# A gate factor held in a ScalarE register, and the o gate's seed copied by VectorE, in a graph layer followed by an LSTM-like cell

## The chip, the cores and the metric

The kernel runs on one core of one Trainium2 chip. The metric is the device time in microseconds of one execution. Before the change the median of three runs is 478.73 us (477.65 to 478.92). One execution was profiled; its span, from the first to the last instruction of the core, is 477.4 us.

## The reference

The input x is 3125 rows of 256 numbers. First comes a graph layer: normalise each row, multiply by a 256 by 256 weight, add a bias, average over the neighbours given by 53,125 (source, destination) pairs, and add to x. Then comes a recurrent cell over the rows as one sequence; its output is added to x again. The cell is what the change touches:

```
i = sigmoid(x_t U_i + b_i + h V_i)      g = tanh(x_t U_c + b_c + h V_c)
o = sigmoid(x_t U_o + b_o + h V_o)
c_new = h * c + i * g                   h_new = o * tanh(c_new)
```

## The kernel before

The 3125 rows are cut into 125 chunks of 25 rows, and the cell advances all 125 chunks side by side: one step of the kernel is one row of every chunk. As the chunks depend on each other only through their ends, the kernel runs 24 early steps with less exact products (`HIDDEN = 24`), mixed into the work of the graph layer, and then 41 full turns (`t` from 25 to `DONE` = 65). At the end a test compares two states and would start a slow path if they did not agree.

A sigmoid is computed as a tanh with halved weights, so all gates use one function. The weights are scaled by a power of two before they are split in two fp16 halves, and each gate's tanh has to undo this factor: it is in the third column of the small tensor `w_unscale`, the same number in all 128 partitions.

In a full turn the 125 chunks are two halves, q = 0 (63 chunks) and q = 1 (62 chunks), which follow each other half a turn apart. I call the work of one half in one turn a half-turn; there are 82. The names and lines of a half-turn, engine by engine:

- TensorE (L1351, function `full_products`): 36 matmuls. The state h is split as hi + lo in fp16. The first 16 take hi for the gates i and g, then 2 for the first part of o, then a wait for `lo_ready`, then 8 matmuls with lo that end i and g (`ig_ps`, these are the 19th to the 26th), then 10 that end o (`o_ps`). The i and g sums of half q are in PSUM bank `ps_g[q]`, the o sum in `ps_x[q]`, four different banks. In the last 25 turns a half-turn also has a transpose of an older state for the output (L1387).
- ScalarE: `gate_ig` (L1024, tanh of i and g, waits for `ig_ps`), `gate_o` (L1032, waits for `o_ps`), `seed_ig` (L1011) and `seed_o` (L1017), which copy the inputs' share `gx` of the half's next turn into the PSUM banks so that the matmuls add to it, and `cell_tanh` (L1038, waits for the new cell `c_ready`).
- VectorE: `new_part` (L1813, i times g, waits for `gate_ig` and for the product h * c), `state_low` of the other half (L1861, writes lo), `cell` (L1819), in the last 25 turns `add_out` (L1883, adds a transposed state to the output), then `state_next`: hi (L1824, output h, waits for the cell's tanh) and the full state (L1824, output h_flat).
- GpSimd: the product h * c (L778).

The order on each engine is that of the Python code; nothing reorders it. In the early steps the gates are L959, for all 125 chunks at once.

The o seed has its place behind both gates and behind the seed of i and g:

Of the kernel before, what the change touches and what calls it, by code (L numbers as in the profile page):

```python
# [6 lines left out]
I32 = mybir.dt.int32  # L7
# [3 lines left out]
ACT = mybir.ActivationFunctionType  # L11
# [14 lines left out]
HIDDEN = 24  # L26
# [7 lines left out]
def bass_gnn_lstm_kernel(nc, x, src, dst, dst_src, w_gnn, b_gnn, U_i, V_i, b_i, U_c, V_c, b_c, U_o, V_o, b_o, out):  # L34
# [4 lines left out]
    HH = H // P  # L39
# [19 lines left out]
    MT = 3 * HH  # L59
# [3 lines left out]
    COLS = [(0, (CHUNKS + 1) // 2), ((CHUNKS + 1) // 2, CHUNKS)]  # L63
# [22 lines left out]
    with ExitStack() as ctx:  # L86
        def sb(name, shape, dt=F32):
            return ctx.enter_context(nc.sbuf_tensor(name, shape, dt))
# [4 lines left out]
        def sem(name):  # L93
            return ctx.enter_context(nc.semaphore(name))
# [8 lines left out]
        gx = gx_flat[:, 0:STEPS * MT * CHUNKS].rearrange("p (s m k) -> p s m k", s=STEPS, m=MT)  # L103
# [89 lines left out]
        w_unscale = sb("w_unscale", [P, 3])  # L193
# [37 lines left out]
        ps_x = [bank[2], bank[3]]  # L231
# [42 lines left out]
        unscales_ready = sem("unscales_ready")  # L274
# [42 lines left out]
        e_gate = sem("e_gate")  # L317
# [20 lines left out]
        o_seed = [sem(f"o_seed{i}") for i in range(2)]  # L338
        ig_gate = [sem(f"ig_gate{i}") for i in range(2)]
        o_gate = [sem(f"o_gate{i}") for i in range(2)]  # L340
# [20 lines left out]
        DONE = 3 * STEPS - RUN * FIRST_GROUP  # L361
# [17 lines left out]
        def at_gx(t):  # L379

            return (t - 1) % STEPS
# [63 lines left out]
        def batch_of(b):  # L445

            return (b // TB, b % TB) if b < TB * PAIRS else (b - PAIRS * (TB - 1), 0)
# [389 lines left out]
        def _(act):  # L837
# [37 lines left out]
            def counts_out(w):  # L875
# [6 lines left out]
                if i == HOT_WINDOWS - 1 and g >= 2:  # L882
# [4 lines left out]
                                         "p (n r t) -> p r t n", n=n, r=RUN),  # L887
                                     ACT.Copy).then_inc(counted, 1)

            act.wait_ge(consts, 1)  # L890
            nc.scalar.activation(sd[0:1, 0:1], ones[0:1, 0:1], ACT.Sqrt).then_inc(table_set, 1)
            act.wait_ge(scales_ready, 1)
            nc.scalar.activation(W16[:, 0, :, :], w_sb[:, 0:DH * D].rearrange("p (d h) -> p d h", d=DH), ACT.Copy,
                                 scale=w_scale[:, 0:1]).then_inc(w_hi, 1)
            nc.scalar.activation(b16[:, :], w_sb[0:B_LOW + 1, DH * D:(DH + 1) * D], ACT.Copy,
                                 scale=w_scale[0:B_LOW + 1, 0:1]).then_inc(b_hi, 1)
# [58 lines left out]
            def early_gate(t, m0, m1):  # L955
                act.wait_ge(e_ps, 2 * t - (1 if m0 == 0 else 0))
                if m0 > 0 and t >= SHARP:
                    act.wait_ge(e_h, t - SHARP + 1)
                nc.scalar.activation(gate_w[:, m0:m1, :],  # L959
                                     ps_early[:, 0:(m1 - m0) * CHUNKS].rearrange("p (m k) -> p m k", k=CHUNKS),  # L960
                                     ACT.Tanh, scale=w_unscale[:, 2:3]).then_inc(e_gate, 1)

            def early_tanh(t):
                of, to = early_cols(t)
# [6 lines left out]
            for w in range(PLACES_END):  # L971
                if w + WINDOWS < NW:
                    counts_out(w + WINDOWS)
                if w == 97:
                    nc.scalar.activation(tc[0:1, 0, 0, 0:1], ones[0:1, 0:1], ACT.Tanh).then_inc(table_set, 1)
                if w in UV_HIGH:
                    if w == UV_HIGH[0]:
                        act.wait_ge(scales_ready, 2)
                    n, u, w_from, w16 = uv_parts[UV_HIGH.index(w)]
                    nc.scalar.activation(w16[:, 0, :, n * H:(n + 1) * H], w_from[:, :, n, :], ACT.Copy,  # L980
                                         scale=w_scale[:, 1 + u:2 + u]).then_inc(uv_hi, 1)
                t = early_turn(w, E_SEED)
                if t:
                    early_seed(t, 0, 2 * HH)
                t = early_turn(w, E_GATE)
                if t:
                    early_gate(t, 0, 2 * HH)
                    early_seed(t, 2 * HH, MT)
                t = early_turn(w, E_OUT_GATE)
                if t:  # L990
                    early_gate(t, 2 * HH, MT)
                t = early_turn(w, E_TANH)
                if t:
                    early_tanh(t)
                for _, (j0, j1), u in gates_at(w, out=True):
                    gates_out(j0, j1 - j0)
                t = block_at(w, HIGH_AT)
                if t is not None:
                    act.wait_ge(z2T_ps, t + 1)
                    batch, at_b = batch_of(t)  # L1000
                    if batch >= 2 and at_b == 0:
                        act.wait_ge(gx_ps, UNITS * (batch - 1))
                    nc.scalar.activation(z2T[:, batch % 2, 0, :, at_b, :],
                                         ps_zT[:, 0:DH * NB].rearrange("p (d n) -> p d n", d=DH),
                                         ACT.Copy).then_inc(z2T_hi, 1)
# [8 lines left out]
            def seed_o(q, s):  # L1014
                c0, c1 = COLS[q]
                n = c1 - c0
                nc.scalar.activation(ps_x[q][:, 0:HH * n].rearrange("p (m k) -> p m k", k=n),  # L1017
                                     gx[:, bass.ds(s, 1), 2 * HH:MT, c0:c1], ACT.Copy).then_inc(o_seed[q], 1)

            def gate_ig(q, turn):  # L1020
                c0, c1 = COLS[q]
                n = c1 - c0
                act.wait_ge(ig_ps[q], turn)
                nc.scalar.activation(gate[:, q, 0:2 * HH, 0:n],  # L1024
                                     ps_g[q][:, 0:2 * HH * n].rearrange("p (m k) -> p m k", k=n), ACT.Tanh,
                                     scale=w_unscale[:, 2:3]).then_inc(ig_gate[q], 1)

            def gate_o(q, turn):
                c0, c1 = COLS[q]
                n = c1 - c0  # L1030
                act.wait_ge(o_ps[q], turn)
                nc.scalar.activation(gate[:, q, 2 * HH:MT, 0:n],  # L1032
                                     ps_x[q][:, 0:HH * n].rearrange("p (m k) -> p m k", k=n), ACT.Tanh,
                                     scale=w_unscale[:, 2:3]).then_inc(o_gate[q], 1)

            def cell_tanh(q, turn, c, c0, c1):
                act.wait_ge(c_ready[q], turn)
# [8 lines left out]
            for t in range(HIDDEN + 1, DONE + 1):  # L1046
                n = t - HIDDEN

                def next_ig(q):
                    if t < DONE:  # L1050
                        act.wait_ge(ig_gate[q], n)
                        seed_ig(q, at_gx(t + 1))

                def tanh_c(q):
                    cell_tanh(q, n, c_after(t), *cols_after(t, q))

                for q in range(2):
                    gate_ig(q, n)
                    gate_o(q, n)
                    next_ig(q)  # L1060
                    if t < DONE:
                        act.wait_ge(o_gate[q], n)
                        seed_o(q, at_gx(t + 1))
                    tanh_c(q)

            def general_block(j):
# [387 lines left out]
        def _(dve):  # L1454
# [318 lines left out]
            for w in range(PLACES_END):  # L1773
# [15 lines left out]
                if w in UV_LOW:  # L1789
                    n = UV_LOW[w]  # L1790
                    m, u, w_from, w16 = uv_parts[n]
# [5 lines left out]
                t = early_turn(w, E_CELL)  # L1797
                if t:
                    early_cell(t)
                t = early_turn(w, E_STATE)  # L1800
                if t:
                    early_state(t)
                t = early_turn(w, E_LOW)
# [23 lines left out]
            def state_next(q, t):  # L1827
# [26 lines left out]
                else:  # L1854
                    state(1, h[:, :, c0:c1], n).then_inc(h_ready[1], 1)

            def state_low(q, t):
                c0, c1 = COLS[q]
                dve.wait_ge(h_ready[q], t - HIDDEN)
                dve.wait_ge(hi_ready[q], t - HIDDEN)  # L1860
                nc.vector.tensor_tensor(h16[:, 1, :, c0:c1], h_after(t)[:, :, c0:c1], h16[:, 0, :, c0:c1],  # L1861
                                        ALU.subtract).then_inc(lo_ready[q], 1)
# [29 lines left out]
            for t in range(HIDDEN + 1, DONE + 1):  # L1892
                n = t - HIDDEN

                def cell_after(q):
                    cell(q, n, c_after(t), *cols_after(t, q))

                if t == LAST_ROUND + 2:
                    dve.wait_ge(x1_stored, 16 * GROUPS_S)
                for q in range(2):  # L1900
                    new_part(q, n)
                    if q == 0 and n > 1:
                        state_low(1, t - 1)
                    elif q == 1 and t < DONE:
                        state_low(0, t)
                    cell_after(q)
                    if (t, q) == (DONE, 1):
                        cell_gap()
                    else:
                        for step, d in out_parts(t, q)[:LAST_OUTS[q]]:  # L1910
                            add_out(step, d)
                    state_next(q, t)
                if n == 1:
                    dve.wait_ge(covered_ps, 1)
                    link(nc.vector.tensor_scalar(open_f[:, :], ps_one[0:1, 0:1], float(E), None, ALU.not_equal))
                    link(nc.vector.tensor_copy(open_i[:, :], open_f[:, :]))
# [127 lines left out]
```

## Time and profile before

| | before |
|---|---|
| median of 3 runs | 478.73 us |
| span of the profiled execution | 477.4 us |
| stage 339.8 to 468.7 us (the full turns) | 128.9 us |
| in it TensorE / ScalarE / VectorE / GpSimd busy | 115.1 / 119.0 / 105.4 / 34.5 us |
| TensorE clock granted over the span | 0.979 |

The file has no time of its own for the profiled execution besides its span; the median of the runs is 1.3 us above that span. Busy times of an engine are sums in which two instructions that overlap count once. An instruction on ScalarE or VectorE may start before the one in front of it has ended, so the distance between two starts is often shorter than the duration of the first. Bracketed notes such as "[0.34 <-PE bank L1351]" give the idle time before an instruction and who ended it. Lines are those of the kernel before.

### The profile page before, as it was taken

To read this page: it belongs to the slowest core of one execution; us is meant where nothing else is said; L and a number is where in the kernel's file an instruction comes from. 1 tells how busy PE (TensorE), PEld (TensorE's weight loads), DVE (VectorE), ACT (ScalarE), POOL (GpSimd) and SP (SyncE) were. 2 spreads that over 40 slices of the span, in tenths; PEclk is the share of its full clock that TensorE was granted. 3 is DMA by queue.
4 is the path that set the end of the run, shared out by engine and by line. 5 is a ranking of instruction groups with operands and counts; after the bars stand their busy time and mean duration, and the time that the engine had idled before them with its cause. 6 is when DMAs were issued, how large, how long until landed. Compare 5 with 4: busy or idle time off the path is not lost.

```text
span 477.4 us, 15480 instructions
## 1 busy us (share of the span) xinstructions
PE 425.7 (89%) x6096; PEld 371.7 (78%) x6096; DVE 356.8 (75%) x1119; ACT 345.6 (72%) x905; POOL 184.8 (39%) x322
## 2 busy tenths in 40 slices
PE   3986988989999999999999999986788889999992
PEld 3674777778888898899988888875677778888882
DVE  4989987897987878778786553345577778888885
ACT  1575786477776777777777755464899989999991
POOL 5730650356454546555464342221122222322320
PEclk9999799999999999999999999997999999999997
DMA  7372001330100001000100010001000000110112
GB/s 190 67 185 84 2 1 43 104 104 24 55 2 1 1 15 42 2 1 7 50 2 2 1 55 1 1 1 56 1 3 3 5 3 4 57 58 3 58 56 61
DMA packets 9604, 16.91 MB, mean 35 GB/s; under 512 B 2006, under 2 KB 7451, under 8 KB 9526
## 3 DMA queue, kind: packets, MB, share of 16 engines
q1 hardware_dynamic: 8230, 14.60, 10.1%
q0 software_dynamic: 880, 0.86, 0.9%
q8 instruction: 50, 0.82, 0.7%
q10 hardware_dynamic: 416, 0.39, 0.3%
q14 instruction: 28, 0.23, 0.2%
HBM read 6.23 MB, written 9.61 MB: 33 GB/s over the span
## 4 chain that ended last, share of the span: by engine, by line
PE 40%; DVE 33%; ACT 13%; issue 7%; POOL 4%; DMA 2%; SPq 0%; DVEq 0%; ACTq 0%
PE bank L1218 9%; PE bank L1220 9%; PE bank L1252 9%; DVE hots L1601 6%; ACT tc L1038 5%; DVE h L1824 5%; DVE h L1861 5%; PE bank L1280 4%; DVE c_st L1819 4%; PE bank L1170 4%; DVE h_flat L1824 3%; POOL newton L744 2%; DMA x_sb<-in_x_dram 2%; ACT counts L885 2%; PE bank L1203 2%
## 5 line engine op out<-in xcount | busy, mean ns | idle before, releaser
L1170 PE MATMUL bank<-hots 128*128 128x125 f16 x625 | 121.1, 223 | 1.7 <-ACT counts L885 1.7
L1351 PE MATMUL bank<-h,V 128*128 128x62 f16 (+1 forms) x2952 | 107.1, 192 | 14.0 <-DVE h L1824 8.7
L1351 PEld LDWEIGHTS bank<-h,V 128*128 128x128 f16 x2952 | 96.4, 97 | 27.9 <-issue 23.3
L1601 DVE TENSOR_TENSOR hots<-iota,kp 128x1024 f16<-128x1024 f16 x160 | 108.9, 710 | 8.8 <-PE bank L1170 8.3
L1218 PE MATMUL bank<-h_flat,counts 125*128 125x257 f16 x375 | 97.2, 273 | 0.4 <-ACT h_flat L873 0.4
L1220 PE MATMUL bank<-h_flat,counts 125*128 125x256 f16 x375 | 96.3, 271 | 0.0
L778 POOL TENSOR_TENSOR hc<-h_flat,c_st 128x126 f32<-128x126 f32 x80 | 34.1, 427 | 97.9 <-DVE c_st L1819 91.5
L885 ACT ACTIVATE counts<-bank 125x500 f16<-125x500 f32 x96 | 55.5, 612 | 19.3 <-PE bank L1170 18.1
L1218 PE MATMUL bank<-h_flat,gx 125*128 125x257 f16 x250 | 68.2, 273 | 0.0
L1220 PE MATMUL bank<-h_flat,gx 125*128 125x256 f16 x250 | 67.4, 270 | 0.0
L1170 PEld LDWEIGHTS bank<-hots 128*128 128x128 f16 x625 | 57.5, 98 | 9.5 <-issue 1.1
L934 ACT ACTIVATE gx<-bank,gb,gx_scale 128x250 f32<-128x250 f32 (+1 forms) x84 | 40.5, 534 | 23.7 <-PE bank L1252 23.6
L1252 PE MATMUL bank<-z2T,U 128*128 128x250 f16 (+1 forms) x504 | 56.7, 261 | 1.0 <-ACT gx L934 0.5
L744 POOL TENSOR_SCALAR newton<-rstd,var_eps 125x1 f32<-125x1 f32 x48 | 30.7, 640 | 66.4 <-DVE rstd L1683 64.0
L885 ACT ACTIVATE gx<-bank 125x500 f16<-125x500 f32 x64 | 37.4, 592 | 19.9 <-PE bank L1170 18.1
L1252 PEld LDWEIGHTS bank<-z2T,U 128*128 128x128 f16 x504 | 44.2, 99 | 6.5 <-issue 1.3
L1218 PEld LDWEIGHTS bank<-h_flat,counts 125*128 125x128 f16 x375 | 36.6, 98 | 4.8 <-issue 0.5
L1824 DVE SCALAR_TENSOR_TENSOR h<-gate,tc 128x126 f16<-128x126 f32 (+1 forms) x80 | 23.6, 295 | 20.6 <-ACT tc L1038 20.6
L1024 ACT ACTIVATE gate<-bank,w_unscale 128x252 f32<-128x252 f32 x82 | 38.5, 470 | 0.3 <-PE bank L1351 0.3
L1220 PEld LDWEIGHTS bank<-h_flat,counts 125*128 125x128 f16 x375 | 36.6, 98 | 1.5
L959 ACT ACTIVATE gate<-bank,w_unscale 128x500 f32<-128x500 f32 (+1 forms) x48 | 27.6, 576 | 13.9 <-PE bank L1280 13.0
L745 POOL TENSOR_SCALAR rstd<-newton,rstd 125x1 f32<-125x1 f32 x48 | 35.7, 744 | 4.9
(169 smaller groups left out, 801.2 us busy)
## 6 DMA issues: line engine op xcount, KB each, us to landing
h_dram<-h_flat SPq DMA_DIRECT2D x1, 3137.2 KB
x_dram<-x_sb SPq DMA_DIRECT2D x5, 625.0 KB
x_sb<-in_x_dram SPq DMA_DIRECT2D x5, 560.0 KB
out_dram<-x_sb SPq DMA_DIRECT2D x4, 560.0 KB
out_dram<-x_sb SPq DMA_DIRECT2D x1, 336.0 KB
x_sb<-in_x_dram SPq DMA_DIRECT2D x5, 65.0 KB
out_dram<-x_sb SPq DMA_DIRECT2D x4, 65.0 KB
gx<-in_L_gnn_weight_dram ACTq DMA_DIRECT2D x1, 256.0 KB, 3.8
```

What stands on the lines that cost most here:

```text
L744: link(nc.gpsimd.tensor_scalar(t, y, v, y, ALU.mult, ALU.mult))
L745: link(nc.gpsimd.tensor_scalar(y, t, -three, y, ALU.add, ALU.mult))
L885: nc.scalar.activation(counts[g % 2][:, :, :, n0:n0 + n], ps_count[group % 3][0:NB, 0:n * KEYS].rearrange("p (n r t) -> p r t n", n=n, r=RUN),
L934: nc.scalar.activation(gx[:, at:at + n, m, :], gates_bank(tile // 2)[:, half * TB * NB:half * TB * NB + n * NB].rearrange("p (s k) -> p s ...
L1024: nc.scalar.activation(gate[:, q, 0:2 * HH, 0:n], ps_g[q][:, 0:2 * HH * n].rearrange("p (m k) -> p m k", k=n), ACT.Tanh, scale=w_unscale[: ...
L1170: nc.tensor.matmul(ps_count[group % 3][:, pos * KEYS:(pos + 1) * KEYS], hots[:, ring, 0, g // 2, :, g % 2], hots[:, ring, 1, g // 2, 0:KEY ...
L1218: nc.tensor.matmul(ps_sum[turn % 2][:, 0:D + 1], of, line[:, s, D:2 * D + 1], start=(s == 0), stop=False, skip_group_check=True)
L1220: return nc.tensor.matmul(ps_sum[turn % 2][:, 0:D], of, line[:, s, 0:D], start=False, stop=(s == BLOCKS - 1), skip_group_check=True)
L1252: mm = nc.tensor.matmul(at_bank[:, half * TB * NB:half * TB * NB + n_blocks * NB], U16[:, w_part, d, m * P:(m + 1) * P], z2T[:, buf, z_par ...
L1351: mm = nc.tensor.matmul(to[:, m % (2 * HH) * n:(m % (2 * HH) + 1) * n], V16[:, v_part, d, m * P:(m + 1) * P], h16[:, h_part, d, c0:c1], st ...
L1601: nc.vector.tensor_tensor(hots[:, k % RING, :, :, :, :].rearrange("p a h n g -> p (a h) n g"), iota[:, :, :].unsqueeze(1).to_broadcast(of) ...
L1824: return nc.vector.scalar_tensor_tensor(out=to, in0=gate[:, q, 2 * HH:MT, 0:n], scalar=1.0, in1=tc[:, q, :, 0:n], op0=ALU.add, op1=ALU.mult)
```

## The change

Three edits. The factor of the gates is loaded once into a register of ScalarE (`reg_load`, just before the switch of the activation table at window 97), behind a wait for the factor, and the three gate instructions take it as a number from the register instead of one number per partition from SBUF. The ScalarE copy `seed_o` is taken out of the loop of the full turns (the two copies before the loop stay). VectorE gets a copy of the same data, directly behind the cell and ahead of `add_out` and `state_next`, behind a wait for the o gate.

```diff
+            gate_scale = act.alloc_register("gate_scale")
...
-                                     ACT.Tanh, scale=w_unscale[:, 2:3]).then_inc(e_gate, 1)
+                                     ACT.Tanh, scale=gate_scale).then_inc(e_gate, 1)
...
                 if w == 97:
+                    act.wait_ge(unscales_ready, 2)
+                    act.reg_load(gate_scale, w_unscale[0:1, 2:3].bitcast(I32))
                     nc.scalar.activation(tc[0:1, 0, 0, 0:1], ones[0:1, 0:1], ACT.Tanh).then_inc(table_set, 1)
...
-                                     scale=w_unscale[:, 2:3]).then_inc(ig_gate[q], 1)
+                                     scale=gate_scale).then_inc(ig_gate[q], 1)
...
-                                     scale=w_unscale[:, 2:3]).then_inc(o_gate[q], 1)
+                                     scale=gate_scale).then_inc(o_gate[q], 1)
...
                     next_ig(q)
-                    if t < DONE:
-                        act.wait_ge(o_gate[q], n)
-                        seed_o(q, at_gx(t + 1))
                     tanh_c(q)
...
+            def seed_o_next(q, t):
+                c0, c1 = COLS[q]
+                n = c1 - c0
+                dve.wait_ge(o_gate[q], t - HIDDEN)
+                nc.vector.tensor_copy(ps_x[q][:, 0:HH * n].rearrange("p (m k) -> p m k", k=n),
+                                      gx[:, at_gx(t + 1), 2 * HH:MT, c0:c1]).then_inc(o_seed[q], 1)
...
                     cell_after(q)
+                    if t < DONE:
+                        seed_o_next(q, t)
                     if (t, q) == (DONE, 1):
```

On ScalarE, a half-turn of half 0 in the full turns, before the change (L1024 and L1032 the gates, L1011 and L1017 the seeds, L1038 the cell's tanh):

```order
L1024 ACTIVATE gate<-bank,w_unscale 128x252 [waits ig_ps0]
L1032 ACTIVATE gate<-bank,w_unscale 128x126 [waits o_ps0]
L1011 ACTIVATE bank<-gx 128x252 [waits ig_gate0]
L1017 ACTIVATE bank<-gx 128x126 [waits o_gate0]
L1038 ACTIVATE tc<-c_st 128x126 [waits c_ready0]
```

And after it, where the same instructions have the lines L1027, L1035, L1014 and L1041:

```order
L1027 ACTIVATE gate<-bank 128x252 [waits ig_ps0]
L1035 ACTIVATE gate<-bank 128x126 [waits o_ps0]
L1014 ACTIVATE bank<-gx 128x252 [waits ig_gate0]
L1041 ACTIVATE tc<-c_st 128x126 [waits c_ready0]
```

The second copy is gone, and the gates no longer read `w_unscale`.

On VectorE, a half-turn of half 1 in the last 25 turns, before the change (L1813 `new_part`, L1861 `state_low` of the other half, L1819 `cell`, L1883 `add_out`, L1824 `state_next`):

```order
L1813 SCALAR_TENSOR_TENSOR ig<-gate 128x2x62 [waits ig_gate1,hc_ready1]
L1861 TENSOR_TENSOR h<-h_flat,h 128x2x63 [waits hi_ready0,h_ready0]
L1819 SCALAR_TENSOR_TENSOR c_st<-hc,ig 128x2x62 [waits ig_ready1]
L1883 SCALAR_TENSOR_TENSOR x_sb<-bank,x_sb 125x128 [waits hT_ready]
L1824 SCALAR_TENSOR_TENSOR h<-gate,tc 128x2x62 [waits tc_ready1]
L1824 SCALAR_TENSOR_TENSOR h_flat<-gate,tc 128x2x62
```

And after it, where L1861 is the new copy, L1868 `state_low` and L1890 `add_out`:

```order
L1813 SCALAR_TENSOR_TENSOR ig<-gate 128x2x62 [waits ig_gate1,hc_ready1]
L1868 TENSOR_TENSOR h<-h_flat,h 128x2x63 [waits hi_ready0,h_ready0]
L1819 SCALAR_TENSOR_TENSOR c_st<-hc,ig 128x2x62 [waits ig_ready1]
L1861 COPY bank<-gx 128x124 [waits o_gate1]
L1890 SCALAR_TENSOR_TENSOR x_sb<-bank,x_sb 125x128 [waits hT_ready]
L1824 SCALAR_TENSOR_TENSOR h<-gate,tc 128x2x62 [waits tc_ready1]
L1824 SCALAR_TENSOR_TENSOR h_flat<-gate,tc 128x2x62
```

The copy stands between the cell and what followed it.

## Rows read from the trace of the kernel before

**Rows 1.** Stages: length, busy us (instructions) of PE, PEld, DVE, ACT, POOL; clock.

```profile
118.00:339.80 221.80, 213.06 (x2313) 190.40 (x2314) 150.73 (x381) 152.53 (x325) 96.43 (x166) 0.98 0.05 16
339.80:468.70 128.90, 115.10 (x2971) 101.13 (x2967) 105.39 (x455) 118.96 (x406) 34.49 (x81) 1.00 0.08 25
```

**Rows 2.** Chain of waits by line, first 398 to 412 us, then 118 to 339.7.

```profile
by line: ACT tc L1038 20.5%; DVE h L1861 20.1%; DVE h L1824 19.0%; issue 15.2%; DVE c_st L1819 13.5%; DVE h_flat L1824 10.3%; DVE ig L1813 3.9%
...
by line: PE bank L1218 19.2%; PE bank L1220 18.8%; PE bank L1252 17.8%; PE bank L1280 9.0%; PE bank L1170 6.9%; DVE hots L1601 4.3%; issue 2.7%; POOL rstd L745 1.9%; ACT bank L952 1.9%; ACT gate L959 1.8%; ACT gx L934 1.7%; PE bank L1228 1.
```

**Rows 3.** ScalarE's timeline over one half-turn: start, duration, instruction.

```profile
348.98 0.31 ACT L1038 ACTIVATE tc<-c_st 128x124 f32<-128x124 f32 x1
349.25 0.47 ACT L1024 ACTIVATE gate<-bank,w_unscale 128x252 f32<-128x252 f32 x1
349.62 0.36 ACT L1032 ACTIVATE gate<-bank,w_unscale 128x126 f32<-128x126 f32 x1
...
350.18 0.28 ACT L1017 ACTIVATE bank<-gx 128x126 f32<-128x126 f32 x1
```

**Rows 4.** VectorE's timeline over the same half-turn.

```profile
348.46 0.28 DVE L1861 TENSOR_TENSOR h<-h_flat,h 128x126 f16<-128x126 f32 x1
...
349.52 0.28 DVE L1824 SCALAR_TENSOR_TENSOR h_flat<-gate,tc 128x124 f32<-128x124 f32 x1
349.82 0.29 DVE L1813 SCALAR_TENSOR_TENSOR ig<-gate 128x126 f32<-128x126 f32 x1
350.03 0.28 DVE L1861 TENSOR_TENSOR h<-h_flat,h 128x124 f16<-128x124 f32 x1
```

**Rows 5.** TensorE's timeline, narrow windows: starts of the 18th, 19th, 26th matmul.

```profile
348.69 0.37 PE L1351 MATMUL bank<-h,V 128*128 128x63 f16 x4
...
348.80 0.35 PE L1351 MATMUL bank<-h,V 128*128 128x63 f16 x6
...
349.02 0.37 PE L1351 MATMUL bank<-h,V 128*128 128x63 f16 x7
```

**Rows 6.** Timeline of the first half-turn; the PE row starts with the 26th matmul.

```profile
339.52 0.37 PE L1351 MATMUL bank<-h,V 128*128 128x63 f16 x7
...
339.75 0.47 ACT L1024 ACTIVATE gate<-bank,w_unscale 128x252 f32<-128x252 f32 x1 [0.34 <-PE bank L1351]
...
340.33 0.29 DVE L1813 SCALAR_TENSOR_TENSOR ig<-gate 128x126 f32<-128x126 f32 x1 [1.19 <-ACT gate L1024]
```

**Rows 7.** All gate_ig of the full turns: count, duration min/median/max ns, first and last start.

```profile
L1024 ACT ACTIVATE gate<-bank,w_unscale x82: 453/470/472, 339.8 to 467.4; 128x252 f32<-128x252 f32 x41, 128x248 f32<-128x248 f32 x41
```

**Rows 8.** Groups of ScalarE by form: busy us, mean ns of one.

```profile
L1032 ACT ACTIVATE gate<-bank,w_unscale 128x126 f32<-128x126 f32 x41 | 14.7, 359 | 0.0
...
L952 ACT ACTIVATE bank<-gx 128x500 f32<-128x500 f32 x24 | 14.3, 596 | 0.0
...
L1038 ACT ACTIVATE tc<-c_st 128x126 f32<-128x126 f32 x41 | 12.7, 311 | 4.9 <-DVE c_st L1819 1.6
L1017 ACT ACTIVATE bank<-gx 128x126 f32<-128x126 f32 x41 | 11.4, 279 | 0.0
...
L980 ACT ACTIVATE V<-gx,w_scale 128x512 f16<-128x512 f32 x3 | 2.1, 713 | 0.0
```

**Rows 9.** VectorE's timeline in a half-turn with an output.

```profile
404.26 0.28 DVE L1819 SCALAR_TENSOR_TENSOR c_st<-hc,ig 128x126 f32<-128x126 f32 x1
404.46 0.28 DVE L1883 SCALAR_TENSOR_TENSOR x_sb<-bank,x_sb 125x128 f32<-125x128 f32 x1
404.92 0.29 DVE L1824 SCALAR_TENSOR_TENSOR h<-gate,tc 128x126 f16<-128x126 f32 x1 [0.18 <-ACT tc L1038]
```

**Rows 10.** ScalarE's register load and register work at the end, then its timeline near 115 us.

```profile
L556 ACTq TENSOR_LOAD <-far_i x1: 468/468/468, 472.1 to 472.1; - x1
...
L556 ACTq FUSED_REGOPS  x1: 167/167/167, 472.6 to 472.6; - x1
...
115.70 0.59 ACT L885 ACTIVATE gx<-bank 125x500 f16<-125x500 f32 x1 [2.26 <-PE bank L1170]
```

## The prediction

> **What bounds the kernel now.** I read the stages first. The change works in the full turns, 128.9 us with no single engine full: TensorE 115.1, ScalarE 119.0, VectorE 105.4 us busy [rows 1]. The stage before, 118 to 339.8 us, is TensorE's (213.1 of 221.8 us) and the change touches it only in the early gates. So the question is what sets the pace of a half-turn. There are 82, whose gates start between 339.8 and 467.4 us [rows 7]: (467.4 - 339.8) / 81 = 1.575 us, and 1.57 for a plain one.
>
> The chain of waits over 398 to 412 us names the cell's tanh, the state, `state_low` and the cell, and no gate at all [rows 2]. By that the gates would be free and the first edit worth nothing. I don't trust it here, because a wait whose releaser ends while the engine is still busy leaves no idle time. So I laid the timelines of one half-turn beside each other and looked for distances that recur.
>
> - `state_low` starts at 348.46 and lasts 0.28, so it ends at 348.74 [rows 4]. The 19th matmul, the first with lo, starts at 348.80, while the 18th started at 348.69 [rows 5]. Within that run matmuls start about 0.03 apart ((349.02 - 348.80) / 7), so the 19th could have come at 348.72: TensorE waits some 0.08 us for lo.
> - The 26th starts at 349.02, the gate at 349.25: 0.23 later [rows 3, 5]. In the first half-turn, where ScalarE sat idle 0.34 us until TensorE was done, it is 339.52 to 339.75, again 0.23 [rows 6]. So the gate starts when TensorE lets it, not when ScalarE is free.
> - The gate ends at 349.25 + 0.47 = 349.72, `new_part` starts at 349.82, 0.10 later. In the first half-turn, with VectorE idle for 1.19 us until the gate, it is 340.22 to 340.33, 0.11 [rows 3, 4, 6]. So `new_part` follows the gate.
> - `new_part` to the next `state_low` 0.21 (350.03), which lasts 0.28 and ends at 350.31 [rows 4].
>
> That closes a loop: 0.06 + 0.22 + 0.23 + 0.47 + 0.10 + 0.21 + 0.28 = 1.57 us, the measured pace. The duration of `gate_ig` is in it, once for each half-turn. The cell, its tanh and the state are a side branch, with little slack.
>
> **Edit 1, the factor from a register.** The trace has no gate with a factor that is not a pointer into SBUF, so I work out what the pointer costs from neighbours [rows 8]. Suppose an ACTIVATE costs a base, plus A for a pointer, S for having both operands in SBUF, T for tanh with its constants.
> - Tanh from PSUM with pointer minus copy into PSUM, 126 elements: T + A = 359 - 279 = 80 ns.
> - Tanh SBUF to SBUF without pointer minus that copy: S + T = 311 - 279 = 32 ns.
> - Copy SBUF to SBUF with pointer at 512 elements, 713, minus the copy into PSUM at 500, 596, plus 12 elements at (596 - 279) / 374 = 0.85 ns: S + A = 713 - 606 = 107 ns.
> So A = (80 + 107 - 32) / 2 = 78 ns. The ends: if S is zero, the tanh pair alone gives 359 - 311 = 48 ns; if the copy pair is all pointer, 107 ns. I take 78, as it fits all three.
>
> The Trainium skill speaks to this ("ScalarE: Activation LUTs", section "What ACT_TABLE_LOAD costs"): an immediate scale and bias take 186 ns + 0.833 ns per element, and each pointer operand adds about 93 ns. By it the saving would be 93 ns per gate, and the sum below would end some 0.5 us lower, since other limits then hold; our 470 ns for 252 elements agrees with it within some 20 ns. It states nothing of a scale in a register.
>
> What is late next, when the loop shrinks? All of the side branch is tied to `new_part`, so its own lengths give floors. TensorE's first 18 matmuls would be the bound 0.08 us below today's pace: 1.57 - 0.08 = 1.49. VectorE could start `new_part` 0.20 behind the full state (it has such a distance between instructions that don't wait, 404.26 to 404.46 [rows 9]); today it is 349.52 to 349.82, 0.30 [rows 4], so the floor there is 1.47. With 78 ns the loop comes to 1.49, just at the first floor: the whole saving is had, and not much more could be. 82 x 0.078 = 6.4 us. With 48 ns it is 3.9, with 107 ns it is cut by the floors to about 0.09 x 82 = 7.4.
>
> `gate_o` gets shorter too, for nothing: its end, 349.62 + 0.36 = 349.98, is long before its readers.
>
> The early gates L959 are 1.8% of the chain over 221.7 us, 4.0 us [rows 2]; at 0.5 to 0.7 us each that is some 7 gates on the path, and 7 x 0.08 = 0.5 us saved. The rest hides behind TensorE.
>
> The register load: the same kind of instruction took 0.47 us on ScalarE's queue at the end. It is put once near 110 us, and soon behind it ScalarE sits idle 2.26 us, until 115.70 [rows 10]. That idle time covers it: cost 0, or at most 0.5 us if TensorE, which needs ScalarE's copies of the counts in between, runs dry. The added wait is for a factor made long before.
>
> **Edit 2, the o seed.** ScalarE loses 0.28 us per half-turn. It ended the seed at 350.18 + 0.28 = 350.46 and only waited for the cell then, so this gives nothing: 0.
>
> VectorE gains a copy of 126 elements from SBUF to PSUM, with no row of its own. Its nearest rows are all 0.28 us long and 0.20 from start to start. Its wait is free: the o gate ends at 349.98, the place of the copy is 0.20 behind the cell, 350.43. Without an output the gap between cell and state is 0.66 us and the copy fits. With an output (50 half-turns) VectorE now has cell, copy, `add_out`, state: 3 x 0.20 = 0.60 against the 0.66 that the state waits anyway (404.92 - 404.26) [rows 9]. It fits with 0.06 to spare: cost 0. If the cover is gone, because the copy holds the next start for the full 0.28 or 0.30, the state comes 0.02 to 0.04 later. TensorE needs the seed only at its 17th matmul of the half's next turn, over 1 us behind the copy. At best the copy gives nothing either; I find no gain in it.
>
> The Trainium skill ("VectorE: DVE Perf Modes", Specifications) says that VectorE sits closer to SBUF and ScalarE closer to PSUM. This speaks against moving a write into PSUM to VectorE; it gives no price, and the first rival below is what it would do.
>
> **The sum.** 6.4 + 0.5 + 0 + 0 = 6.9 us off the profiled span of 477.4, so 470.5; the median of the runs is 1.3 above the span, so 471.8. I forecast 472.0.
>
> **Rivals.**
> - *VectorE becomes the bound in the half-turns with an output.* The copy holds VectorE 0.30 instead of 0.20, hi comes 0.04 late, TensorE's 18 matmuls too, and their floor goes from 1.49 to 1.53: 50 x 0.04 = 2.0 us given back, 474.0. For it: only 0.06 of slack, a write to PSUM. Against: every VectorE row here, reading PSUM or not, has the 0.20.
> - *The pointer costs only 48 ns.* 3.9 + 0.3 = 4.2 us saved, 474.5. For it: the only pair of tanh rows. Against: then the pointer in the copies would cost over twice as much. Together with the rival above it ends near 476.5.
> - *The change doesn't do what it says.* A factor from a register costs the engine what a pointer did, and the gate stays at 470 ns: 478.5, no change. No row excludes it.
> - *Slower.* ScalarE's sequencer has to fetch and place the register's value for each gate after the wait for TensorE, in the loop's path. Its register work at the end took 0.167 us [rows 10]. Then each half-turn has 0.167 - 0.078 = 0.09 more, 82 x 0.09 = 7.3 us, 486. It decides from a fetch of 0.078 us on. For it: the gates wait right there, so nothing hides it. Against: that row is a group of register operations, not an operand.
>
> **How the numbers follow.** Forecast 0.57, VectorE bound 0.14, small pointer 0.15, no effect 0.06, slower 0.08. A change of 0.3%, 1.4 us, is about what a measurement here can tell from none. Faster: 0.57 + 0.14 + 0.15 = 0.86; same 0.06; slower 0.08. The range: below, 107 ns cut by the floors, 7.4 + 0.8 = 8.2, gives 470.5, and I go to 470.2 for a full loop at 1.47; above, both of the first rivals, 476.5.
>
> **What would show it.** In the profile after, `gate_ig` lasts about 0.39 us and the distance of two of them is 1.49; the 19th matmul follows the 18th at nearly its normal distance; `new_part` still follows the gate's end by 0.10; the copy lasts about 0.28, the next start on VectorE is 0.20 behind it, and the state still follows the cell's start by 0.66 with an output. The gate at 0.42 would be the second rival, at 0.47 the third; a longer distance than 0.23 from the 26th matmul to the gate the fourth; a state 0.70 behind the cell the first. I am wrong at the root if the gate gets shorter and the pace stays.

## The result and the profile after

The changed kernel takes 471.53 us (median of 4 runs, 471.05 to 472.93) against 478.5 us before. The ratio is 0.9847, 95% interval 0.9823 to 0.987: faster by 7 us. 472.0 was forecast. The span of the profiled execution is 469.7 us, its own time 471.51.

The two long stages, in the columns of [rows 1]:

```profile
118.00:338.70 220.70, 212.04 (x2313) 190.01 (x2312) 150.49 (x381) 148.28 (x325) 97.28 (x166) 0.99 0.05 16
338.70:461.00 122.30, 109.06 (x2972) 97.63 (x2968) 114.33 (x535) 90.45 (x325) 34.48 (x81) 1.00 0.08 25
```

The full turns went from 128.9 to 122.3 us. ScalarE lost 29 us of busy time there and VectorE gained 9, but neither number is the gain; the next rows are. All of `gate_ig`, which answers to [rows 7], and all of `gate_o`:

```profile
L1027 ACT ACTIVATE gate<-bank x82: 361/381/382, 338.7 to 460.1; 128x252 f32<-128x252 f32 x41, 128x248 f32<-128x248 f32 x41
...
L1035 ACT ACTIVATE gate<-bank x82: 266/276/278, 339.0 to 460.4; 128x126 f32<-128x126 f32 x41, 128x124 f32<-128x124 f32 x41
```

The gate went from 470 to 381 ns, 89 ns less. From the first gate to the last it is now 460.1 - 338.7 = 121.4 us, where it was 127.6. A half-turn at the same place in time as in [rows 3 to 5], after the change (there the gate is half 0's, here half 1's). ScalarE's timeline:

```profile
348.99 0.31 ACT L1041 ACTIVATE tc<-c_st 128x126 f32<-128x126 f32 x1 [0.36 <-DVE c_st L1819]
349.25 0.38 ACT L1027 ACTIVATE gate<-bank 128x248 f32<-128x248 f32 x1
```

VectorE's (L1861 is the copy, L1868 `state_low`):

```profile
348.27 0.29 DVE L1813 SCALAR_TENSOR_TENSOR ig<-gate 128x126 f32<-128x126 f32 x1
348.47 0.28 DVE L1868 TENSOR_TENSOR h<-h_flat,h 128x124 f16<-128x124 f32 x1
348.67 0.29 DVE L1819 SCALAR_TENSOR_TENSOR c_st<-hc,ig 128x126 f32<-128x126 f32 x1
348.87 0.29 DVE L1861 COPY bank<-gx 128x126 f32<-128x126 f32 x1
349.34 0.29 DVE L1824 SCALAR_TENSOR_TENSOR h<-gate,tc 128x126 f16<-128x126 f32 x1 [0.18 <-ACT tc L1041]
349.54 0.28 DVE L1824 SCALAR_TENSOR_TENSOR h_flat<-gate,tc 128x126 f32<-128x126 f32 x1
349.74 0.28 DVE L1813 SCALAR_TENSOR_TENSOR ig<-gate 128x124 f32<-128x124 f32 x1
```

TensorE's, in narrow windows, with the starts of the 18th, the 19th and the 26th matmul:

```profile
348.77 0.35 PE L1351 MATMUL bank<-h,V 128*128 128x62 f16 x6
...
348.81 0.35 PE L1351 MATMUL bank<-h,V 128*128 128x62 f16 x6
...
349.02 0.34 PE L1351 MATMUL bank<-h,V 128*128 128x62 f16 x6
```

Three things are to be seen. The pace is 349.74 - 348.27 = 1.47 us. The 19th matmul follows the 18th by 0.04 where it was 0.11 [rows 5], so TensorE no longer waits for lo by anything to speak of. And `new_part` follows the full state by 0.20 where it was 0.30 [rows 4]: VectorE goes from one to the next without a pause, while the gate's end (349.25 + 0.38 = 349.63) is also still only 0.11 ahead. The gate's loop, TensorE's first 18 matmuls and VectorE's own row are now nearly equally long. The loop alone, 1.565 less the gate's 0.089, gives 1.476, and the distance of two gates is 1.479 in the median (1.565 before).

In a half-turn with an output, to be set beside [rows 9]:

```profile
398.63 0.28 DVE L1819 SCALAR_TENSOR_TENSOR c_st<-hc,ig 128x124 f32<-128x124 f32 x1
398.83 0.28 DVE L1861 COPY bank<-gx 128x124 f32<-128x124 f32 x1
399.02 0.28 DVE L1890 SCALAR_TENSOR_TENSOR x_sb<-bank,x_sb 125x128 f32<-125x128 f32 x1
399.28 0.29 DVE L1824 SCALAR_TENSOR_TENSOR h<-gate,tc 128x124 f16<-128x124 f32 x1
```

The copy lasts 0.28, the next instruction starts 0.19 behind it, and the state comes 399.28 - 398.63 = 0.65 behind the cell, as before the change (0.66).

What was not foreseen is a short stall of VectorE. Here the distance from `new_part` to `state_low` is 0.46 and not 0.20, and no one is named as its cause:

```profile
383.97 0.29 DVE L1813 SCALAR_TENSOR_TENSOR ig<-gate 128x126 f32<-128x126 f32 x1
384.43 0.29 DVE L1868 TENSOR_TENSOR h<-h_flat,h 128x124 f16<-128x124 f32 x1 [0.17 <-issue]
```

The list of waits from 340 to 465 us counts them, first after, then before the change (waiting line, releaser, us in total, times, longest):

```profile
DVE h L1868 <- issue: 0.5, 3, 0.2
```

```profile
DVE h L1861 <- issue: 0.2, 1, 0.2
```

There are three after and one before. Each makes its half-turn 0.25 us longer.

### The profile page after: what moved, and what is told of

It is laid out like the page before. It is cut to its first block, busy times and chain, and to the rows that moved or that the text cites. A ratio compares the mean times of both kernels' runs of the same rounds, so it can differ in the third digit from the quotient of the medians.

```text
span 469.7 us, 15481 instructions
## 1 busy us (share of the span) xinstructions
PE 417.7 (89%) x6096; PEld 367.2 (78%) x6096; DVE 365.8 (78%) x1199; ACT 312.9 (67%) x825; POOL 186.2 (40%) x322
## 4 chain that ended last, share of the span: by engine, by line
PE 40%; DVE 35%; ACT 10%; issue 7%; POOL 4%; DMA 2%; SPq 0%; DVEq 0%; ACTq 0%
PE bank L1218 9%; PE bank L1220 9%; PE bank L1252 9%; DVE hots L1601 6%; DVE h L1824 5%; DVE h L1868 5%; PE bank L1280 4%; DVE c_st L1819 4%; PE bank L1170 4%; ACT tc L1041 2%; DVE bank L1861 2%; DVE x_sb L1890 2%; DMA x_sb<-in_x_dram 2%; POOL newton L744 2%; ACT counts L885 2%
## 5 line engine op out<-in xcount | busy, mean ns | idle before, releaser
L1351 PE MATMUL bank<-h,V 128*128 128x62 f16 (+1 forms) x2952 | 101.1, 192 | 13.9 <-DVE h L1824 8.7
L1351 PEld LDWEIGHTS bank<-h,V 128*128 128x128 f16 x2952 | 92.9, 97 | 25.2 <-issue 23.0
L744 POOL TENSOR_SCALAR newton<-rstd,var_eps 125x1 f32<-125x1 f32 x48 | 31.8, 662 | 65.7 <-DVE rstd L1683 63.3
L1041 ACT ACTIVATE tc<-c_st 128x126 f32<-128x126 f32 x82 | 25.4, 309 | 32.1 <-DVE c_st L1819 32.1
L745 POOL TENSOR_SCALAR rstd<-newton,rstd 125x1 f32<-125x1 f32 x48 | 36.8, 766 | 4.9
L758 POOL TENSOR_TENSOR hc<-h,c_st 128x250 f32<-128x250 f16 x20 | 18.9, 944 | 39.6 <-DVE h L1749 38.6
L1280 PE MATMUL bank<-h,V 128*128 128x125 f16 x348 | 28.7, 224 | 6.6 <-ACT bank L953 4.6
```

The costliest lines, as they stand in the source:

```text
L744: link(nc.gpsimd.tensor_scalar(t, y, v, y, ALU.mult, ALU.mult))
L745: link(nc.gpsimd.tensor_scalar(y, t, -three, y, ALU.add, ALU.mult))
L1041: nc.scalar.activation(tc[:, q, :, 0:c1 - c0], c_st[:, c, :, c0:c1], ACT.Tanh, scale=0.5).then_inc(tc_ready[q], 1)
L1280: mm = nc.tensor.matmul(ps_early[:, (m - m0) * CHUNKS:(m - m0 + 1) * CHUNKS], V16[:, v_part, d, m * P:(m + 1) * P], h16[:, h_part, d, :], ...
L1351: mm = nc.tensor.matmul(to[:, m % (2 * HH) * n:(m % (2 * HH) + 1) * n], V16[:, v_part, d, m * P:(m + 1) * P], h16[:, h_part, d, c0:c1], st ...
```

## The experiments

Theory A is the loop of the prediction: `state_low`, 8 matmuls with lo, `gate_ig`, `new_part`. Its rivals: B, ScalarE's total work counted and so the copy's removal did; C, the copy hurts VectorE; D, the chain of waits is right and the gate has slack; E, a register costs a part of the pointer's price. "Before" is the kernel before, run on the same chip in turn; its median is 479.41 us beside the first four experiments and 478.56 beside the last four, where it was 478.5 beside the changed kernel. So ratios compare better than medians. Every profile is of one execution. Distances called medians are over the half-turns of one profile.

### Edit 1 alone

```diff
   kernel before, and:
-  ACT.Tanh, scale=w_unscale[:, 2:3])     # L959, L1024, L1032
+  ACT.Tanh, scale=gate_scale)            # with the register and its load
```

> All gates take the factor from the register, the o seed stays on ScalarE (edit 1 alone). Theory A (the loop state_low, 8 matmuls, gate_ig, new_part sets the pace, the copy on VectorE gives nothing): the pace of a plain half-turn is 1.476 us as in the changed kernel, and the time is that of the changed kernel, 471.5 us, or up to 0.5 us less, as VectorE then has fewer instructions and perhaps fewer of the stalls of 0.25 us seen in the changed kernel's row of half-turns. Theory B (the copy's removal from ScalarE is part of the gain): the time lies 1 us or more above 471.5. Theory C (VectorE is hurt by the copy in the half-turns with an output): over 1.5 us below 471.5.

472.57 us, ratio to before 0.9858, interval 0.983 to 0.9887; the changed kernel has 0.9847. So the gain is there without edit 2, to within what the times can tell. But by its words the expectation was missed: 472.57 is 1.07 us above 471.5, and 1 us or more was to speak for theory B. The kernel before ran 0.9 us slower beside it too, and in the profile the excess lies ahead of the full turns, which start at 340.6 us and not at 338.7. The gate:

```profile
L1027 ACT ACTIVATE gate<-bank x82: 361/380/382, 340.6 to 461.5; 128x252 f32<-128x252 f32 x41, 128x248 f32<-128x248 f32 x41
```

From first to last gate 120.9 us, 0.5 less than in the changed kernel, and one stall where that has three. In the median times this is not seen. The pace is 1.476 in the median, as expected. In the full turns theory A holds and B falls, and the next two experiments test B again; C, which wanted over 1.5 us below 471.5, falls by the time.

### Edit 2 alone

```diff
   changed kernel, and:
-  scale=gate_scale)
+  scale=w_unscale[:, 2:3])
```

> The o seed is copied by VectorE, the gates keep the pointer (edit 2 alone). Theory A: gate_ig lasts 470 ns, the pace stays 1.566 us, the time is that of the kernel before, 478.5 us, within 0.7 us. Theory B (ScalarE was the bound and the second copy's 0.28 us counted): 2 us or more faster than before.

478.99 us, ratio 1.0, interval 0.9981 to 1.0019: nothing. The first and last gate start at 338.9 and 467.2, which is 128.3 us against 127.6 before, and the list of waits again has three stalls:

```profile
L1024 ACT ACTIVATE gate<-bank,w_unscale x82: 453/472/474, 338.9 to 467.2; 128x252 f32<-128x252 f32 x41, 128x248 f32<-128x248 f32 x41
...
DVE h L1865 <- issue: 0.5, 3, 0.2
```

So by the profiles the copy costs some 0.6 us, and it buys nothing. It is too little for the times to tell.

### The register for gate_o alone

```diff
   kernel before, with the register and its load, and only in gate_o:
-  scale=w_unscale[:, 2:3]).then_inc(o_gate[q], 1)
+  scale=gate_scale).then_inc(o_gate[q], 1)
```

> Only gate_o of the full turns takes its factor from the register; gate_ig and the early gates keep the pointer. Theory A: gate_o gets 0.08 to 0.09 us shorter, 82 times, and the time does not move (478.5, within 0.7 us), because nothing on the path waits for it. Theory B (ScalarE's total time counts): about 0.08 x 82 = 6.6 us faster would need ScalarE to be full; a part of it, over 1.5 us, would speak for B.

478.74 us, ratio 0.9992, interval 0.9975 to 1.001. `gate_o` got 92 ns shorter in the median (266 ns, it was 358), 82 times, 7.5 us of ScalarE's work, and the time stayed:

```profile
L1035 ACT ACTIVATE gate<-bank x82: 262/266/268, 339.1 to 466.7; 128x126 f32<-128x126 f32 x41, 128x124 f32<-128x124 f32 x41
```

The same 90 ns are worth 7 us in one gate and nothing in the other. That excludes B once more.

### A second pointer on gate_ig

```diff
   kernel before, and in gate_ig:
+  bias=no_bias[:, 0:1],                   # 128 x 1 zeros in SBUF
   scale=w_unscale[:, 2:3]).then_inc(ig_gate[q], 1)
```

> The kernel before, with one pointer more on gate_ig: a bias of zeros from SBUF. Theory A (the gate's duration is in the loop once per half-turn): gate_ig gets 0.09 us longer, 0.56 us, the pace becomes 1.566 + 0.09 = 1.656 us and the time 478.5 + 82 x 0.09 = 485.9 us. Theory D (the chain of waits is right and the gate has slack): less than 2 us slower.

486.71 us, ratio 1.0167, interval 1.0133 to 1.02: slower by 7.3 us against the median beside it, 8 by the ratio; 7.4 were expected.

```profile
L1027 ACT ACTIVATE gate<-bank,no_bias,w_unscale x82: 546/563/565, 338.2 to 473.2; 128x252 f32<-128x252 f32 x41, 128x248 f32<-128x248 f32 x41
```

The gate is 93 ns longer, and first to last gate is 135.0 us, 7.4 more than before (82 x 0.093 = 7.6). The pace is 1.659 in the median, where 1.656 was expected. The gate's duration goes into the time one to one. D falls: the chain of waits before the change, which named no gate [rows 2], was misleading.

### The kernel before with two waits swapped

```diff
             def new_part(q, turn):
-                dve.wait_ge(hc_ready[q], turn)
                 dve.wait_ge(ig_gate[q], turn)
+                dve.wait_ge(hc_ready[q], turn)
```

> The kernel before, with the two waits of new_part in the other order: the one for gate_ig is written first, so that the wait for the product of GpSimd, long done, becomes the separate instruction, and the gate's wait stands on new_part itself. The gate keeps its pointer. Theory A: the 0.10 us from the gate's end to new_part are in the loop. They are 0.04 to the separate wait, 0.02 of it, 0.04 behind it; with the wait on the instruction itself 0.03 to 0.06 should be left, as from the cell's tanh to the state (0.03). The pace falls from 1.566 to about 1.50 us and the time by 82 x 0.06 = 5 us, to about 474. Theory D (the gate has slack): no change.

472.64 us, ratio 0.9875, interval 0.9853 to 0.9897. Two lines in another order, with the pointer left in, give 6 us; 5 were expected. From first to last gate it is 122.2 us (338.1 to 460.3), 5.4 less than before. ScalarE's gate and VectorE's `new_part`:

```profile
347.29 0.47 ACT L1024 ACTIVATE gate<-bank,w_unscale 128x252 f32<-128x252 f32 x1
...
348.79 0.47 ACT L1024 ACTIVATE gate<-bank,w_unscale 128x248 f32<-128x248 f32 x1
```

```profile
347.56 0.28 DVE L1824 SCALAR_TENSOR_TENSOR h_flat<-gate,tc 128x124 f32<-128x124 f32 x1
347.80 0.29 DVE L1813 SCALAR_TENSOR_TENSOR ig<-gate 128x126 f32<-128x126 f32 x1
```

From the gate's end (347.76) to `new_part` it is 0.04 where it was 0.10. The pace is the distance of two gates, 348.79 - 347.29 = 1.50 us, as expected from the loop. Another link of the loop was cut, and the time followed.

### The changed kernel with the same swap

```diff
   changed kernel, and the swap of the experiment above
```

> The changed kernel with the same swap. Theory A with floors: in the changed kernel the 19th matmul no longer waits (29 ns behind the 18th) and new_part stands 0.20 behind the full state, so TensorE and VectorE hold the pace at 1.47 to 1.48 us whatever the gate does; the same 0.06 us off the gate's path now gives under 1 us: 470.5 to 471.5. If instead the gate alone still set the pace, it would fall to 1.41 and the time to 466.

471.01 us, ratio 0.9833 to before, interval 0.9805 to 0.986; the changed kernel's is 0.9847. The same 0.06 us that gave 6 us now gives nothing that the times can tell. In the profile the first and last gate start at 339.6 and 459.8, which is 1.2 us less than in the changed kernel: no stall of `state_low` is in its list of waits, and the pace is 1.474 in the median, not 1.41. VectorE shows why:

```profile
348.71 0.29 DVE L1824 SCALAR_TENSOR_TENSOR h<-gate,tc 128x124 f16<-128x124 f32 x1 [0.18 <-ACT tc L1041]
348.92 0.28 DVE L1824 SCALAR_TENSOR_TENSOR h_flat<-gate,tc 128x124 f32<-128x124 f32 x1
349.12 0.28 DVE L1813 SCALAR_TENSOR_TENSOR ig<-gate 128x126 f32<-128x126 f32 x1
```

The distances are 0.20 throughout. From the gate's end to `new_part` it is again 0.10 in the median, though 0.03 would be enough: the gate has slack, and the side branch of the prediction sets the pace: cell, tanh, state, full state, `new_part`, `state_low`, cell.

### The factor as a number

```diff
   changed kernel without the register, and for these inputs:
-  scale=gate_scale)
+  scale=2.0 ** -17)
```

> The changed kernel with the gates' factor as a number in the instruction, the power of two that these inputs give, and no register. Theory A: the register is read for nothing, gate_ig lasts 380 ns as with the register, the distance from the 26th matmul to the gate stays 0.23, the time stays within 0.7 us of the changed kernel. Theory E (a register costs a part of the pointer's price): gate_ig under 370 ns or the distance under 0.22.

469.48 us, ratio 0.9806, interval 0.9767 to 0.9845; its interval overlaps that of the changed kernel (0.9823 to 0.987). The gate:

```profile
L1024 ACT ACTIVATE gate<-bank x82: 360/380/381, 337.1 to 458.6; 128x252 f32<-128x252 f32 x41, 128x248 f32<-128x248 f32 x41
```

It lasts as long as with the register, and 458.6 - 337.1 = 121.5 us from first to last is that of the changed kernel, 121.4. From the 26th matmul to the gate it is 0.23 in the median, as with the register. Reading the register costs nothing in the full turns, E falls. The median is 2 us lower than the changed kernel's, which is outside the 0.7 us that were expected; in the profile that difference lies ahead of the first gate (337.1 against 338.7). It goes with TensorE's clock. The stage ahead is TensorE's, and near its end the granted clock of the changed kernel is at half (1.2 GHz) for 3.4 us, 330.0 to 333.4, with TensorE busy all the while; the mean from 326 to 336 us is 0.83, and here it is 1.00. Half the work of 3.4 us is 1.7 us, and from the first early gate to the first gate of the full turns it is 220.1 us in the changed kernel and 218.4 here. The sizes agree, but this is the only profile without the dip, so it is not shown that none of the 1.7 us is the register's. First the stretch of the changed kernel, then 326 to 336 us here, in the columns of [rows 1]:

```profile
330.00:333.40 3.40, 3.40 (x34) 3.40 (x34) 1.31 (x3) 0.36 (x2) 0.63 (x1) 0.50 0.06 20
```

```profile
326.00:336.00 10.00, 5.71 (x90) 5.00 (x88) 5.84 (x17) 6.68 (x17) 1.05 (x3) 1.00 0.14 54
```

### A version made from what was learnt

```diff
   edit 1 alone, the swap in new_part, and:
             def full_products(q, turn, hi_seen, lo_seen):
-                pe.wait_ge(ig_seed[q], turn)
                 ... wait for hi_ready[q] ...
+                pe.wait_ge(ig_seed[q], turn)
...
             def state_low(q, t):
                 dve.wait_ge(h_ready[q], t - HIDDEN)
-                dve.wait_ge(hi_ready[q], t - HIDDEN)
```

> A version made from what the runs showed: the register for all gates, the o seed back on ScalarE (fewer instructions on VectorE, so fewer of its stalls), the waits of new_part swapped, the two waits at the head of a half's matmuls swapped so that the one for hi stands on the first matmul (0.146 us from the state's end now, against 0.057 for lo), and in state_low one of its two waits left out, as the later instruction's covers the earlier one. Theory A with floors: TensorE's floor falls below VectorE's, which is 0.66 + 4 x 0.20 = 1.46 us; the pace goes from 1.476 to 1.46, 1 to 1.5 us less, and one stall fewer gives 0.3 to 0.5: 469.5 to 470.5 where the changed kernel has 471.5.

469.95 us, ratio 0.9827, interval 0.9801 to 0.9854; span 466.9. First to last gate 119.7 us, 1.7 less than the changed kernel:

```profile
L1027 ACT ACTIVATE gate<-bank x82: 361/381/383, 337.8 to 457.5; 128x252 f32<-128x252 f32 x41, 128x248 f32<-128x248 f32 x41
```

The pace is 1.471 in the median, where 1.46 was expected. The first matmul now starts 0.057 us behind the state's end (0.146 before) and the 19th waits for lo again, 0.089 behind the 18th, so TensorE's first matmuls have slack, and the pace stayed where it was with the swap alone: VectorE sets it. No stall of `state_low` is left in its list of waits. By the median it is the better of the two by 1.6 us, but its interval overlaps that of the changed kernel, so only the profile says that it is faster. The swap in `new_part` alone had brought 1.2 of the 1.7 us. What gives the other 0.5, the copy back on ScalarE or one of the two edits of waits, was not tried.

## Why the prediction was right

**The loop.** It was read against the chain of waits, from distances that recurred where an engine had sat idle. The fourth experiment adds 93 ns to the gate and gets 7.4 us between first and last gate; the fifth takes 0.06 us from another link and gets the pace of 1.50. This is shown.

**The price of the pointer.** This term was mis-sized: 78 ns were taken from a range of 48 to 107, and it is 89 on `gate_ig` (470 to 381), 90 on the early gates (574 to 484 in the median) and 93 as a second pointer. The 93 ns of the Trainium skill ("ScalarE: Activation LUTs", section "What ACT_TABLE_LOAD costs") is the better number; these three agree with it within 4 ns. On `gate_o` it is 92 behind a `gate_ig` with pointer (358 to 266) but 82 behind one without (276), so one gate's duration also depends on what runs ahead of it. The weak step was to let three kinds of operations share one additive cost: T, which the sum needed at about 2 ns, comes out at 276 - 279 = -3 from `gate_o` without pointer against the copy, or at 266 - 279 = -13, and the copy with pointer pulled the estimate down.

**The floors.** They entered the range and not the sum: 1.49 for TensorE's first 18 matmuls and 1.47 for VectorE. TensorE's was wrong: the pace is 1.476 to 1.479 with the register and 1.474 with the swap added. The wait of 0.08 for lo was read rightly, but using it up doesn't stop the pace there: those matmuls hang on a state that follows `new_part` and so a gate, and it comes earlier too when the gates get shorter. In the changed kernel the wait is gone, the 19th matmul follows the 18th at 0.029 in the median, which is their normal distance, and the pace fell by 0.086 all the same. VectorE's floor of 1.47 is real: the sixth experiment reaches it while the gate has slack, and the last one stays on it with slack at TensorE too. In the changed kernel no floor took more than a few ns off the saving; the forecast was near because a price 11 ns too low moves it by only 0.9 us (82 x 0.089 = 7.3 against 6.4), most of which other terms took back.

**The copy.** Cost 0 and gain 0 were forecast. Gain 0 is shown by the first two experiments. The price in place was right, 0.28 us with 0.20 from start to start, and VectorE did not become the bound through it. What no row showed are the two more stalls, 0.5 us. With the waits of `new_part` in their old order they go with the copy: three in the changed kernel, in edit 2 alone and with the factor as a number, one in the kernels without the copy. With the two waits swapped none is listed, not even where the copy stays. What VectorE does in them the profile doesn't say, and the cause is open.

**Where 6.2 us come from.** 81 distances at 0.086 us, the fall of the median, are 7.0 us. Three half-turns (the third, and the 32nd and 33rd, where all 25 rows of the chunks are done and the states move on to the next chunk; 1.75 to 1.9 us long) are held by other waits and gave nothing, 0.3 us. The two stalls take 0.5. The forecast of 6.4 for this part was good in part by luck: the price was too low, and these losses were not foreseen.

**The rest.** The register load lasted 0.47 us as forecast, from 109.2 us on. ScalarE's engine was then still busy with the instruction ahead, and the table load followed at once, so it cost nothing:

```profile
L977 ACTq TENSOR_LOAD <-w_unscale x1: 472/472/472, 109.2 to 109.2; - x1
```

```profile
109.30 0.58 ACT L885 ACTIVATE gx<-bank 125x500 f16<-125x500 f32 x1
109.91 1.28 ACT L978 ACT_TABLE_LOAD   x1
```

The 0.5 us for the early gates came out as forecast, once profiles with the same clock are compared. Near 330 us TensorE's granted clock is at half (1.2 GHz) in all profiles but one, for 3.4 or 6.8 us, and both lengths occur with either kind of gate. From the first early gate to the first gate of the full turns, with the granted clock from 326 to 336 us:

| clock | early gates with pointer | from the register |
|---|---|---|
| 0.66 | 221.0 (before), 221.1 (`gate_o` only) | 220.3 (edit 1 alone) |
| 0.83 | 220.5 (edit 2 alone), 220.4 (second pointer), 220.5 (swap) | 220.1 (changed), 220.0 (with the swap), 220.1 (last version) |

That is 0.3 to 0.5 us for the register at 0.83 and 0.7 to 0.8 at 0.66. The spans fell by 7.7 us, 477.4 to 469.7: 6.2 between the first gate and the last, 0.9 in this stage, of which 0.3 to 0.5 are the gates and the rest the clock, 0.2 ahead of it, and 0.4 behind the last gate, a stretch that varies by 0.8 over the profiles. The last two and the clock's part are luck for a forecast of 6.9.

**The rivals.** The small pointer and the one without effect are excluded by 381 ns. The slower one is excluded too: from the 26th matmul to the gate it is 349.25 - 349.02 = 0.23 us, as with the pointer [rows 3, 5], so no fetch stands in the path. The VectorE one is excluded by the 0.65 us from cell to state.

## What to carry to other kernels

When a chain of waits leaves out an engine that is always busy just before its reader, check the distance from its end to the reader's start against a place where the reader sat idle: if they are equal, the engine is in the loop. Then add up the loop and the side branches, because the longest of the others says how much a cut can bring; here two quite different edits each brought 6 to 7 us, and both together 7.5. Of several waits ahead of one instruction, write the one that comes last in time first, and see in the trace that it stands on the instruction itself.

## What the runs showed of the hardware

The place of a wait matters. Of two waits ahead of one instruction the one written last stood as a separate instruction (21 ns) in these traces. When that is the late one, VectorE's `new_part` starts 0.102 us behind the gate's end in the median; with the late wait on the instruction itself (fifth experiment) it is 0.033. On TensorE the same exchange brought a half's first matmul from 0.146 to 0.057 us behind the end of the state (last experiment). The 0.06 to 0.07 us on VectorE are some three quarters of the 0.089 that the pointer of the gate costs, and they gave 6 us without touching any arithmetic.

A factor from a register costs ScalarE what a number in the instruction costs: 381 against 380 ns, with 0.23 us from the 26th matmul to the gate in both.
